# An attention and expert-routing kernel on one core: the second head's q copies, q's low tile and the split-weight stores move from SyncE to GpSimd

## The reference

```python
xn = _layernorm(x)                                   # 8 x 512 x 256
Q = jnp.einsum('bse,hec->bhsc', X, Wq) + bq          # 16 heads, 2 maps of 64 each
K = jnp.einsum('bse,hec->bhsc', X, Wk) + bk
V = jnp.einsum('bse,hed->bhsd', X, Wv) + bv
A1, A2 = Q1 @ K1.T * s, Q2 @ K2.T * s                # the two maps of a head
P = softmax(A1) - lam * softmax(A2)
O = P @ V
attn = layernorm(concat(O) @ Wo + bo) * gamma * 0.2 + beta * 0.2
ffn = the expert of argmax(t @ switch_w + switch_b), gelu between w1 and w2, times its probability
out = x + attn + ffn
```

## Time and profile before

| what | value |
|---|---|
| median of three runs | 1816.8 us (1815.08 to 1817.29) |
| the profiled execution's own time | 1819.72 us |
| its span | 1817.9 us |
| PE busy | 1777.5 us, 98% |
| DVE busy | 1542.1 us, 85% |
| ACT busy | 1423.3 us, 78% |
| POOL busy | 639.0 us, 35% |
| DMA, mean rate | 239 GB/s, most of it on SP's queue |

### The profile page before, as it was taken

The page is one execution under the profiler, slowest core; times in us unless marked ns, Lnnn a source line. Parts: engine busy times, 40 slices in busy tenths (PEclk is TensorE's granted clock), DMA queues, the critical chain, the costliest instruction groups (busy, mean ns, idle before and its releaser), DMA issues. The chain is left out here.

```text
span 1817.9 us, 33121 instructions
## 1 busy us (share of the span) xinstructions
PE 1777.5 (98%) x10714; PEld 1362.8 (75%) x10714; DVE 1542.1 (85%) x2636; ACT 1423.3 (78%) x3364; POOL 639.0 (35%) x711
## 2 busy tenths in 40 slices
PE   6999999999999999999999999999999999999997
PEld 5666667777777677777777677777777689999997
DVE  4988898898889988988898889888999866887667
ACT  4998888888888888888888888888888876677622
POOL 2443222322222222222322322322226546552255
PEclk8999999999999999999999999999999999999999
DMA  8998988898889888988898898888887676667797
GB/s 245 245 252 244 246 233 227 230 248 232 224 230 245 228 226 231 249 231 225 239 239 231 221 241 241 231 221 221 224 208 200 191 263 249 238 237 259 273 368 286
DMA packets 212120, 435.05 MB, mean 239 GB/s; under 512 B 29584, under 2 KB 107152, under 8 KB 203888
## 3 DMA queue, kind: packets, MB, share of 16 engines
q1 hardware_dynamic: 207104, 418.94, 82.7%
q0 software_dynamic: 4688, 13.51, 2.3%
q10 hardware_dynamic: 160, 0.52, 0.1%
HBM read 175.17 MB, written 49.15 MB: 123 GB/s over the span
## 5 line engine op out<-in xcount | busy, mean ns | idle before, releaser
L629 ACT ACTIVATE e<-p_score,nmax 128x512 f32<-128x512 f32 x1024 | 697.2, 688 | 123.3 <-DVE nmax L976 115.7
L976 DVE TENSOR_REDUCE nmax<-p_score 128x2 f32<-128x1024 f32 x512 | 623.1, 1217 | 149.9 <-PE p_score L1135 120.6
L493 POOL TENSOR_SCALAR e<-e,rrec,lam 128x512 f32<-128x512 f32 x512 | 394.0, 769 | 977.4 <-DVE rrec L943 977.0
L1135 PE MATMUL p_score<-ks,qs 128*128 128x512 f32 x1608 | 450.1, 402 | 10.4 <-DMA ks<-k_parts 8.2
L1089 PE MATMUL p_proj<-xh,w 128*128 128x512 f32 x1024 | 386.2, 418 | 6.6 <-DVE k_parts L918 5.2
L581 ACT COPY pT<-p_tr 128x512 f32<-128x512 f32 x512 | 302.9, 592 | 104.3 <-PE p_tr L1147 98.9
L950 DVE SCALAR_TENSOR_TENSOR pm<-e,rrec 128x512 f32<-128x512 f32 x512 | 383.2, 749 | 0.4 <-POOL e L493 0.2
L1135 PEld LDWEIGHTS p_score<-ks,qs 128*128 128x128 f32 x1608 | 292.4, 189 | 85.1 <-DMA ks<-k_parts 10.4
L1147 PEld LDWEIGHTS p_tr<-consts,pm 128*128 128x128 f32 x2048 | 241.7, 140 | 104.2 <-issue 39.6
L1147 PE MATMUL p_tr<-consts,pm 128*128 128x128 f32 x2048 | 315.1, 276 | 1.4 <-ACT pT L581 1.4
L1164 PE MATMUL p_pv<-pT,v 128*64 128x512 f32 x1024 | 247.8, 605 | 0.7 <-ACT pT L581 0.7
(11 more groups left out here) (219 smaller groups left out, 2029.8 us busy)
## 6 DMA issues: line engine op xcount, KB each, us to landing
ks<-k_parts SPq DMA_DIRECT2D x510, 256.0 KB, 5.0
qs<-q_parts SPq DMA_DIRECT2D x512, 128.0 KB, 4.7
w<-weight_parts_scratch SPq DMA_DIRECT2D x56, 1024.0 KB, 10.7
w<-in_w SPq DMA_DIRECT2D x46, 1024.0 KB, 7.3
oT_parts_scratch<-oT SPq DMA_DIRECT2D x32, 512.0 KB, 6.7
op<-oT_parts_scratch SPq DMA_DIRECT2D x16, 1024.0 KB, 9.4
wv<-weight_parts_scratch SPq DMA_DIRECT2D x56, 256.0 KB, 5.5
weight_parts_scratch<-w SPq DMA_DIRECT2D x8, 1024.0 KB, 5.8
```

The source lines that it names most:

```text
L493: nc.gpsimd.tensor_scalar(e2, e2, rrec[:, g % 4, 1:2], lam[:, 0:1], ALU.mult, ALU.mult).then_inc(s_e2, 1)
L629: nc.scalar.activation(ex[:, g % EX, m, :], p_score[g % 2][:, m, :], ACT.Exp, bias=nmax[:, g % 2, m:m + 1], accum_out=rsum[:, g % 4, m:m + ...
L976: vec.tensor_reduce(nmax[:, g % 2, :], p_score[g % 2][:, :, :], AXX, ALU.max, negate=True).then_inc(s_max, 1)
L1135: last_op = nc.tensor.matmul(p_score[g % 2][:, m, :], qs[j][u][:, m, qt * P:(qt + 1) * P], ks[j][u][:, m, part, :], start=(part == 0), sto ...
```

## The change

SP keeps the copies of k and those of the first head's q. POOL issues the second head's four q copies, both `q_low` copies and the two stores of `store_w`. The second head's q gets a semaphore of its own, `s_qdup`, for which PE waits (beside `s_dup`) ahead of the second head's first scores, and ACT before it writes that tile again. On POOL the first head's `q_low` copy stands after e2 of `st` 3, the second head's four copies and its `q_low` after e2 of `st` 5, and the stores after e2 of `st` 7; for pair 0 all of them and the stores of pairs 0 and 1 stand ahead of the loop. Two entries of `ROUTE_OPS` change: three operations at g = 462 and none at g = 463, where it was two and one.

```diff
-ROUTE_OPS = (1,) * 8 + (0, 0, 2, 1) + (2,) * 8 + (1,) * 6 + (2,) * 2 + (1,) * 5
+ROUTE_OPS = (1,) * 8 + (0, 0, 3, 0) + (2,) * 8 + (1,) * 6 + (2,) * 2 + (1,) * 5
...
+        s_qdup = [sem(f"a_qdup{j}") for j in range(2)]
...
-        DUPS = 8
+        DUPS, POOL_DUPS = (8, 4), 4
...
                         queue.dma_start(qs[j][u][half * D:(half + 1) * D, m, :].bitcast(F32),
-                                        a[:, part, :].bitcast(F32)).then_inc(s_dup[j][u], 16)
-                    if m == 1 and by_rows(pair):
-                        queue.dma_start(q_low[j][u][:, :].bitcast(F32), src[:, 1, ROWS_AT:ROWS_AT + P].bitcast(F32)
-                                        ).then_inc(s_low[j][u], 16)
+                                        a[:, part, :].bitcast(F32)).then_inc(s_dup[j][u] if u == 0 else s_qdup[j], 16)
...
-            for what in "qk":
-                spread(1, what, 0)
+            spread(1, "k", 0)
...
-            store_w(0)
-            store_w(1)
...
-                if pair + 1 < NPAIRS:
-                    spread(1, "q", pair + 1)
                 if pair + 4 < PAIRS:
                     load_raw_v(pair + 4)
-                if pair + 2 < PAIRS:
-                    store_w(pair + 2)
...
+            def store_w(pair):
+                j = pair % 2
+                pool.wait_ge(s_wvlo, pair + 1)
+                pool.dma_start(wp_d[pair, :, :, WQK:WPAIR].rearrange("p a (k d) -> p a k d", d=P),
+                             wv[pair // 2 % 2][:, :, :, j * P:(j + 1) * P].bitcast(F32)).then_inc(s_wst[j], 16)
+                pool.wait_ge(s_wqlo, 2 * pair + 2)
+                pool.dma_start(wp_d[pair, :, :, 0:WQK], w[j][:, :, :].bitcast(F32)).then_inc(s_wst[j], 16)
+
+            def send_q_low(u, pair):
+                j = pair % 2
+                pool.wait_ge(s_lo, 4 * pair + 2 * u + 1)
+                pool.dma_start(q_low[j][u][:, :].bitcast(F32), parts["q"][u][:, 1, ROWS_AT:ROWS_AT + P].bitcast(F32)
+                               ).then_inc(s_low[j][u], 16)
...
+            send_q_low(0, 0)
+            pool.wait_ge(s_lo, 3)
+            spread_by(pool, 1, "q", 0)
+            send_q_low(1, 0)
+            store_w(0)
+            store_w(1)
...
+                if pair + 1 < NPAIRS and by_rows(pair + 1) and st == 3:
+                    send_q_low(0, pair + 1)
+                if pair + 1 < NPAIRS and st == 5:
+                    pool.wait_ge(s_lo, 4 * (pair + 1) + 3)
+                    spread_by(pool, 1, "q", pair + 1)
+                    if by_rows(pair + 1):
+                        send_q_low(1, pair + 1)
+                if pair + 2 < PAIRS and st == 7:
+                    store_w(pair + 2)
...
-                    act.wait_ge(s_dup[1 - j][u], 16 * DUPS * ((pair - 1) // 2 + 1))
+                    act.wait_ge(s_dup[1 - j][u], 16 * DUPS[u] * ((pair - 1) // 2 + 1))
+                    if what == "q1":
+                        act.wait_ge(s_qdup[1 - j], 16 * POOL_DUPS * ((pair - 1) // 2 + 1))
...
-                    pe.wait_ge(s_dup[j][u], 16 * DUPS * (pair // 2 + 1))
+                    pe.wait_ge(s_dup[j][u], 16 * DUPS[u] * (pair // 2 + 1))
+                    if u == 1:
+                        pe.wait_ge(s_qdup[j], 16 * POOL_DUPS * (pair // 2 + 1))
```

7 lines of the change are left out of this document (removed).

## The result

The change made the kernel slower. The median of twenty runs went from 1815.86 to 1820.81 us; the ratio is 1.0027, 95% interval 1.0019 to 1.0035, about +4.95 us. The profiled execution took 1824.17 us (span 1822.4), so it is 3.4 us above its median, as that of the kernel before was 2.9 above the one it was given with.

What follows compares the result with a forecast made beforehand. PE, busy 98% of the span, was taken as the bound, so its idle gaps cost time. Terms -5.2 - 4.6 - 1.35 + 4.4 = -6.8 us gave 1810.0 us; the range given was 1805 to 1822.

Steps and rivals of the forecast that it cites:

- pair 0, store earlier: Pair 0: weight store issued earlier on POOL, ACT waits 1.3 us instead of 4.8, PE's gap shrinks by 3.5; gain 5.2 us.
- SP no longer late, pairs 5 and 7: Pairs 5 and 7: SP, rid of issues, sends k copies earlier and PE's waits for them go; gain 4.6 us.
- routing: At g = 464: the eleventh routing operation moves earlier, so PE's idle time before the projection goes; gain 1.35 us.
- POOL blocked, first pairs: Pairs 0 to 5: e2 of st 6 comes 2.19 us late behind issues and a weight's split; 4.4 us lost.
- steady pairs, POOL blocked; q later: Steady pairs: e2 of st 6 is 0.93 us late, within PE's 1.45 us; later q still lands in time; cost 0.
- 1.7 us for the half clock: After PE's long gaps in pairs 0 and 5: 3.4 us at half clock, claimed to cost 1.7 us each.
- my DMA rival: First pairs: DMA engines, not SP's issuing, are late, so 4.6 us of gain fail; 1814.7 us, no change; chance 0.25.
- the slack: Pair 34: scores start 1.45 us after the exponents they need; claimed as time PE has to spare when e2 is late.
- The dear issue: POOL's issues cost over 0.85 us each, so every pair pays; near 1820 us, 1861 at 1.01 us; chance 0.18.
- my 0.20: Whole kernel: the chance given to a slower result.

Runs made afterwards that it cites:

- e2: Not a run but a name of code: the tile of POOL's tensor_scalar instruction in each st, for which DVE's combination waits; it has no measured time or ratio.

## Why the prediction was wrong

I forecast 1810.0 us, faster; it is 1820.8, slower. The terms, beside what the means of three profiles of either kernel show:

| term | predicted | measured |
|---|---|---|
| pair 0, store earlier | -5.2 | -0.2 (27.9 against 28.1 us) |
| SP no longer late, pairs 5 and 7 | -4.6 | -1.9 |
| routing | -1.35 | -1.5 |
| POOL blocked, first pairs | +4.4 | +7 |
| steady pairs, POOL blocked; q later | 0 | +3.5 |

The lines on SP and on POOL in the first pairs split the stretch of pairs 1 to 6: waits for k copies (with 1.7 us for the half clock in the first profile) are 2.4 us in the mean before and 0.5 after, and the rest of the stretch is 131.7 and 138.7 us. With -0.1 for pair 7 the loop is 6.6 us longer in these means, and the spans 5.0; what lies behind pair 58 is 1.6 us shorter, but it varies from 472.3 to 476.1 us among three profiles of the kernel before, so I draw nothing from it.

*The store of pair 0* failed at the step "On SP it took 40.15 - 33.71 = 6.44 us from issue to ACT's start; by that ACT goes on at 36.67." From 29.59 it took 9.93 us. I gave a DMA a fixed duration where the DMA share was 1.05 (from 29.59 to 39.52). Issuing earlier moved a start, not the bytes in front: SP, rid of the q copies, issued its x loads earlier as well. With the q copies back on SP, which put the x loads behind the store (from 32.66 on, the store at 27.68), ACT waited 2.33 us; with the store ahead of the x loads on SP 2.69; with the x loads held until the store had landed 0. The move to another issuer took 4.12 us off the issue and 0.6 off ACT's start. The rule that I cited for my DMA rival, from the Trainium skill ("DMA: Bandwidth & Descriptors", Issuing engines are not separate DMA queues), held in this place, where I had not applied it. The 1.7 us for the half clock failed by itself too: in pair 0 it cost nothing that shows, as the run with the routing alone has it.

*SP late* was right in kind and too large. The pair 5 wait is gone in all three profiles of the changed kernel, as forecast. But 2.06 us and its half clock were the longest of four such waits, three of them in unchanged kernels and one with the routing alone changed. The profiled execution was 2.9 us over the median, I said so, and then took its waits as typical.

*Routing* was right, in place and size.

*POOL blocked in the first pairs*: the price was lower than taken (0.536 us for a copy, 0.56 to 0.61 for `q_low`), which by my own sum left no loss: 72.87 + 0.77 + 2.7 + 1.28 = 77.6, 1.2 us late and under the slack of 1.45. The loss came all the same. The failed step is that I counted only POOL's time: moving the subtraction also put it on top of DVE operations with two operands in SBUF, and DVE stood. This is 3 us of the 7; 2 us more go when the four copies leave POOL (from 135.4, with either move of the subtraction, to 133.3, without the waits before pair 7), and the rest, about 1.5, is the slow pair 1 that is left then, with its half clock; what brought on its gap I did not take apart. I wrote that the slack might be smaller than in pair 34; that it was is shown by the combination's idle time, 5.9 us in four places.

*POOL blocked in a steady pair* was right at 0: e2 is not late behind the five issues. What failed is the sentence "The second head's q is issued later than by SP [...] and even with the longest landing of 8.7 us it is there". True, and beside the point: I asked when the moved copies land, and not what their later issue does to other transfers. PE waited for the first head's k, which SP issues four steps later: 1.2 to 4.6 us in the three profiles, while the stretch is 3.5 us longer in the mean. That the time of issue decides is shown (1827.4 against 1819.1 us for 2.7 us of it); the path to the k copies is not.

*The rivals.* The dear issue is out (0.54, far under 0.85). Its mechanism was shown by the copies at `st` 3, where a wait took the place of the price. "No change: the DMA engines are late" named the resource, but only as something that keeps a gain away; that fuller queues could cost something I had not made a case of. The measured time lies inside the range, on the side of my 0.20, but by luck: that end of the range stood for dear issues, and they were cheap.

Four things stay open: what held L766, and the combination at the end of pair 4, before POOL's subtraction began; by which path late q copies delay the first head's k; why POOL's copies from pair 8 on cost more alone (11 us) than with those of the first pairs; and how much of the wait behind late copies on SP is SP's.

## What to carry to other kernels

When a DMA is moved to another engine, ask three things: when it is issued against when its data are ready, which transfers the engine that is rid of it will now issue earlier beside it, and on which instructions of the neighbour engine the displaced compute now falls. A wait found in one profile is a sample: take a second profile before a term of the sum rests on it, above all when that execution is slower than the median. A store that others wait for goes ahead of loads that nobody needs yet; here that, with the stores on POOL and the new routing table, gave 0.14%, and of the places tried the q copies were best left on SP.
